# A hybrid attention block: first stacks and values loaded inside the projection, attention's results kept by token, the memory stage's first batch loaded inside attention

## What is computed

```python
qk = x @ w_attn.T + b_attn                      # x is the normalised input, v = x
q, k, v = (_heads(q), _heads(k), _heads(x))     # 16 heads of 8
scores = where(causal, einsum('bhqd,bhkd->bhqk', q, k) * scale, -inf)
y_ar = einsum('bhqk,bhkd->bhqd', softmax(scores), v)
e  = v[:, :, 1:, :] - y_ar[:, :, :-1, :]
qa = -leaky_relu(-q[:, :, 1:, :] * scale, 0.02)
ka = sigmoid(_heads(x[:, :-1] @ w_k2.T + b_k2) * scale * 0.02)
y_ma = einsum('bhqk,bhkd->bhqd', where(strictly_causal, qa @ ka.T, 0), e)
out = merge(y_ar) @ w_proj.T + merge(y_ma) @ w_proj.T + 2 * b_proj
```

## Time and profile before

| what | value |
|---|---|
| median of three runs | 1926.33 us |
| profiled execution | 1940.25 us, span 1938.2 us |
| TensorE busy | 1394.9 us (72%) |
| VectorE busy | 1283.7 us (66%) |
| GpSimd busy | 863.3 us (45%) |
| ScalarE busy | 833.6 us (43%) |
| mean granted TensorE clock | 0.829 of full speed |
| projection | 0 to 88.5 us |
| attention | 88.5 to 628.6 us |
| memory stage | 628.6 to 818.8 us |

### The profile page before, as it was taken

How to read it: one execution, slowest core, us unless ns; L and a number is a source line. 1 busy time by engine, 2 the same in 40 slices (tenths; PEclk the granted TensorE clock), 3 DMA queues, 4 the chain that set the end, 5 groups by cost and what they waited for, 6 DMA issues and landing times. The chain is left out here.

```text
span 1938.2 us, 29318 instructions
## 1 busy us (share of the span) xinstructions
PE 1394.9 (72%) x8975; PEld 721.5 (37%) x8976; DVE 1283.7 (66%) x2982; ACT 833.6 (43%) x1181; POOL 863.3 (45%) x761
## 2 busy tenths in 40 slices
PE   4459999999998488767598557586686545481992
PEld 1113333333332366644497222131131101351992
DVE  4567888888983144476233259999999998571333
ACT  3305666666666011122254267557466332120551
POOL 3401111121122333367366316876868665473662
PEclk9657999999999587878799778788797666796996
DMA  4721111111100765153232367785957763534335
GB/s 136 233 78 40 44 61 43 54 52 42 61 9 10 110 122 99 40 160 108 59 94 78 104 168 185 195 211 146 233 147 188 191 163 76 161 94 115 88 93 147
DMA packets 232076, 214.96 MB, mean 111 GB/s; under 512 B 66079, under 2 KB 201218, under 8 KB 229634
## 3 DMA queue, kind: packets, MB, share of 16 engines
q1 hardware_dynamic: 209934, 184.90, 37.6%
q0 software_dynamic: 9216, 19.02, 3.0%
q10 hardware_dynamic: 12800, 9.46, 1.6%
HBM read 149.46 MB, written 63.37 MB: 110 GB/s over the span
## 5 line engine op out<-in xcount | busy, mean ns | idle before, releaser
L772 ACT ACTIVATE attn_prob<-attn_ps_cols 128x1024 f32<-128x1024 f32 (+1 forms) x320 | 290.5, 940 | 231.1 <-PE attn_ps_cols L648 229.8
L2298 POOL TENSOR_TENSOR ssm_hc<-ssm_h,ssm_cb 128x1024 f32<-128x1024 f32 x128 | 301.4, 2356 | 169.8 <-DVE ssm_h L2281 122.3
L2281 DVE TENSOR_TENSOR_SCAN ssm_h<-ssm_decay,ssm_ps_u 128x1024 f32<-128x1024 f32 x128 | 292.6, 2286 | 17.2 <-DVE ssm_ps_u L2276 0.5
L798 POOL TENSOR_SCALAR_AFFINE_SELECT attn_prob<-attn_prob 128x512 f32<-128x512 f32 x128 | 81.2, 635 | 428.2 <-ACT attn_prob L772 428.2
L680 DVE CUSTOM_DVE_ANT_0 attn_ps_rows<-attn_ps_rows,const_mask_rows 128x384 f32<-128x384 f32 (+3 forms) x512 | 235.4, 521 | 42.6 <-PE attn_ps_rows L615 42.5
L615 PE MATMUL attn_ps_rows<-attn_ks,attn_qs 72*128 72x512 bf16 (+3 forms) x768 | 228.3, 351 | 42.3 <-DMA attn_qs<-parts_dram 29.1
L2232 PE MATMUL ssm_ps_u<-ssm_stack,ssm_spread 96*128 96x512 bf16 x256 | 100.3, 484 | 175.7 <-DVE ssm_h L2281 170.3
L2269 ACT ACTIVATE ssm_decay<-ssm_wide,ssm_aneg 128x1024 f32<-128x1024 f32 x128 | 146.0, 1146 | 179.0 <-DVE ssm_h L2281 120.6
L648 PE MATMUL attn_ps_cols<-attn_qs,attn_ks 75*128 75x512 bf16 (+3 forms) x768 | 194.4, 333 | 4.9 <-DMA attn_qs<-attn_nrows 4.1
L667 PE MATMUL attn_ps_o<-attn_prob,attn_vw 128*32 128x512 f32 (+3 forms) x1536 | 166.6, 506 | 0.3 <-POOL attn_prob L798 0.3
L685 DVE TENSOR_REDUCE attn_nm<-attn_ps_rows 128x1 f32<-128x512 f32 x256 | 157.7, 680 | 7.8 <-PE attn_ps_rows L615 7.8
(11 more groups left out here) (321 smaller groups left out, 2471.1 us busy)
## 6 DMA issues: line engine op xcount, KB each, us to landing
ssm_wide<-delta_dram SPq DMA_DIRECT2D x128, 512.0 KB, 6.4
attn_ks<-parts_dram SPq DMA_DIRECT2D x48, 192.0 KB
attn_qs<-parts_dram SPq DMA_DIRECT2D x48, 192.0 KB
parts_dram<-proj_parts SPq DMA_DIRECT2D x8, 768.0 KB, 3.8
ffn1e_x<-ex_dram SPq DMA_DIRECT2D x40, 130.0 KB, 2.3
ffn2e_x<-ex_dram SPq DMA_DIRECT2D x40, 130.0 KB, 2.2
split_dram<-ssm_parts SPq DMA_DIRECT2D x6, 768.0 KB, 4.4
ssm_stack<-split_dram SPq DMA_DIRECT2D x18, 256.0 KB, 4.3
```

What stands on the lines that cost most here:

```text
L772: nc.scalar.activation(prob[u % RING][:, heads[0]:heads[-1] + 1, 0:w], ps_cols[s % 2][:].rearrange("p b (x q) -> p (b x) q", x=len(heads) ...
L2281: nc.vector.tensor_tensor_scan(h[t % H_RING][:], decay[t % DECAY_RING][:], ps_u[t % 2][:], 0.0, ALU.mult, ALU.add).then_inc(scan_done, 1)
L2298: nc.gpsimd.tensor_tensor(hc[:, t % HC_RING, :], h[t % H_RING][:], cb[b % 2][:], ALU.mult).then_inc(hc_done, 1)
```

## The change

Three things are done. First, `qs`, `ks`, `vc` and their semaphores live in a holder `Lead` made before the projection. SP issues the stacks of groups 0 and 1 and the values of groups 0 and 1 between the last stores of the projection. Second, `yar` has the shape 4096 x 128, a row to a token: each `y` store writes 128-byte pieces 512 bytes apart, and `yt` is loaded by one DMA of 512-byte pieces. Third, a holder `Early` has the memory stage's weights and the buffers of its first batch. They are loaded by SP behind group 12 (weights, `kr`, `qr`) and group 13 (`kaT`, `yt`, `vs`, `qaT`, `x`). Besides, a stack is loaded one column step later (`cols_done` at `g * SPG + 1`).

```diff
+class Lead:
+    def __init__(self, nc, ctx):
+        self.m = m = Mem(nc, ctx, "lead")
+        self.qs = [m.sb(f"qs{k}", [SROWS, GH, T], BF16) for k in range(STACKS)]
+        self.ks = [m.sb(f"ks{k}", [SROWS, GH, T], BF16) for k in range(STACKS)]
+        self.vc = [m.sb(f"vc{k}", [P, BLK, GH * (HD + 1)]) for k in range(2)]
...
+    def load_stack(self, sp, dram, g, k):
...
+        for s in range(PARTS):
+            at = s * PARTS * HD
+            sp.dma_start(self.ks[k][at:at + PARTS * HD], split[1][g]).then_inc(self.k_loaded[k], 16)
+            sp.dma_start(self.qs[k][at:at + PARTS * HD],
+                         split[0][g, s].unsqueeze(0).broadcast_to([PARTS, HD, GH * T])).then_inc(self.q_loaded[k], 16)
...
                     store_parts(B - 2 + k // 2, k % 2)
+                    if k == 0:
+                        for half in range(2):
+                            sp.wait_ge(parts_stored[half], 16)
+                    if k < 2:
+                        lead.load_stack(sp, dram, k, k)
+                    if k == 2:
+                        for half in range(2):
+                            sp.wait_ge(vp_stored[half], 16)
+                            lead.load_values(sp, dram, half, half)
...
-        yar = dram["yar"].rearrange("g (c j p) n -> g c p j n", c=2, p=P)
+        yar = dram["yar"].rearrange("(b c j p) (g n) -> b g c p j n", b=B, c=2, p=P, g=GPB)
...
             if stack:
-                sp.wait_ge(cols_done, g * SPG)
+                sp.wait_ge(cols_done, g * SPG + 1)
...
-                load_stack(sp, 0, 0)
-                for k in range(2):
-                    sp.dma_start(vc[k][:], vp[0, k]).then_inc(v_loaded[k], 16)
-                load_stack(sp, 1, 1)
                 sp.wait_ge(ones_ready, 1)
...
+                    if g == GROUPS - 4:
+                        early.load_weights(sp, a)
+                        early.load_rows(sp, dram)
+                    if g == GROUPS - 3:
+                        for ch in range(2):
+                            sp.wait_ge(y_stored[ch], GPB * 16)
+                        early.load_tokens(sp, dram, a)
...
-            for g in range(GPB):
-                sp.dma_start(yt[k][:, :, g * GH * HD:(g + 1) * GH * HD], yar[i, g]).then_inc(y_loaded[k], 16)
+            sp.dma_start(yt[k][:], dram["yar"][i * T:(i + 1) * T, :].rearrange("(j p) d -> p j d", p=P)).then_inc(y_loaded[k], 16)
...
-                for i in range(B):
+                for i in range(1, B):
                     load_batch(sp, i)
```

More of the change, by code:

```diff
@@ L24 @@
 KROWS = COMBOS * HD
+SROWS = KROWS + PARTS
+STACKS = 4
 MROW = 96
@@ L549, in bank_free, with __init__, load_rows, load_weights @@
     return nth(g, same[-1] if same else -1)
-def attention(nc, dram, c):
+RTILES = 4
+class Early:
+    def __init__(self, nc, ctx):
+        self.m = m = Mem(nc, ctx, "early")
+        self.wrow, self.brow = m.sb("wrow", [P, P]), m.sb("brow", [P, P])
+        self.qr, self.kr = m.sb("qr", [P, GH, T]), m.sb("kr", [P, GH, T])
+        self.kaT, self.qaT = m.sb("kaT", [P, T]), m.sb("qaT", [P, T])
+        self.yt, self.vs, self.x = (m.sb(n, [P, BLK, D]) for n in ("yt", "vs", "x"))
+        self.w_loaded = m.sem("w_ld")
+        self.r_loaded, self.y_loaded, self.v_loaded, self.ka_loaded, self.qa_loaded, self.x_loaded = (
+            m.sem(n) for n in ("r_ld", "y_ld", "v_ld", "ka_ld", "qa_ld", "x_ld"))
+    def load_rows(self, sp, dram):
+        feature = [dram["fT"][q].rearrange("(g d r) (b t) -> b r d g t", g=GPB, d=HD, b=B) for q in range(2)]
+        for r in range(RTILES):
+            sp.dma_start(self.kr[32 * r:32 * r + HD], feature[1][0, r]).then_inc(self.r_loaded, 16)
+            sp.dma_start(self.qr[32 * r:32 * r + HD], feature[0][0, r]).then_inc(self.r_loaded, 16)
+    def load_weights(self, sp, a):
+        sp.dma_start(self.wrow[:], a["w_proj"]).then_inc(self.w_loaded, 16)
+        sp.dma_start(self.brow[:], a["b_proj"].rearrange("(o n) -> o n", o=1).broadcast_to([P, P])).then_inc(self.w_loaded, 16)
+    def load_tokens(self, sp, dram, a):
+        sp.dma_start(self.kaT[:], dram["fT"][1, :, 0:T]).then_inc(self.ka_loaded, 16)
+        sp.dma_start(self.yt[:], dram["yar"][0:T, :].rearrange("(j p) d -> p j d", p=P)).then_inc(self.y_loaded, 16)
+        sp.dma_start(self.vs[:], dram["xn"][1:T + 1, :].rearrange("(j p) d -> p j d", p=P)).then_inc(self.v_loaded, 16)
+        sp.dma_start(self.qaT[:], dram["fT"][0, :, 0:T]).then_inc(self.qa_loaded, 16)
+        sp.dma_start(self.x[:], a["x"][0:T, :].rearrange("(j p) d -> p j d", p=P)).then_inc(self.x_loaded, 16)
@@ L555, in attention @@
+def attention(nc, dram, c, lead, early, a):
     with ExitStack() as ctx:
         m = Mem(nc, ctx, "attn")
-        qs = [m.sb(f"qs{k}", [SROWS, GH, T], BF16) for k in range(STACKS)]
-        ks = [m.sb(f"ks{k}", [SROWS, GH, T], BF16) for k in range(STACKS)]
+        qs, ks, vc, q_loaded, k_loaded, v_loaded = lead.qs, lead.ks, lead.vc, lead.q_loaded, lead.k_loaded, lead.v_loaded
         ones = m.sb("ones", [PARTS, GH * T], BF16)
-        vc = [m.sb(f"vc{k}", [P, BLK, GH * (HD + 1)]) for k in range(2)]
@@ L574, in attention @@
         filled, passed, ones_ready, ones_stored = (m.sem(n) for n in ("filled", "passed", "ones_ready", "ones_st"))
-        q_loaded, k_loaded = ([m.sem(f"{n}{k}") for k in range(STACKS)] for n in ("q_ld", "k_ld"))
-        v_loaded, v_wide = m.pair("v_ld"), m.sem("v_wide")
+        v_wide = m.sem("v_wide")
         rows_done, rows_free = m.sem("rows_done"), m.sem("rows_free")
@@ L831, in _ @@
                     sp_group(sp, g, g % 4, g > 0, g + 1 < GROUPS, g + 3 < GROUPS,
[L832 removed]
+                             g + 2 < GROUPS)
+                    if g == GROUPS - 4:
[5 more added lines that the diff above has]
+                        early.load_tokens(sp, dram, a)
                 store_y(sp, GROUPS - 1, 1, nth(GROUPS - 1, RPP - 1) + 1)
@@ L879, in attention @@
         m.leave()
+        lead.m.leave()
 HALF = BLK // 2
-RTILES = 4
 AM_RING = 2
@@ L1182, in memory @@
         m.leave()
+        early.m.leave()
 EXPERTS, HIDDEN, TOP = 8, 256, 2
@@ L2627, in build @@
         routing_scratch(nc, m, dram, ("ffn1", "ffn2"))
-        project(nc, dram, c, {"x": rows, "w_attn": w_attn, "b_attn": b_attn, "w_k2": w_k2, "b_k2": b_k2})
-        attention(nc, dram, c)
-        memory(nc, dram, c, {"x": rows, "w_proj": w_proj, "b_proj": b_proj})
+        with ExitStack() as held:
+            early, rest = Early(nc, held), {"x": rows, "w_proj": w_proj, "b_proj": b_proj}
+            with ExitStack() as led:
+                lead = Lead(nc, led)
+                project(nc, dram, c, {"x": rows, "w_attn": w_attn, "b_attn": b_attn, "w_k2": w_k2, "b_k2": b_k2}, lead)
+                attention(nc, dram, c, lead, early, rest)
+            memory(nc, dram, c, early, rest)
         ffn(nc, dram, c, experts, "ffn1", dram["x1"], None)
```

61 lines of the change are left out of this document (28 added, 33 removed).

## The result

The kernel after the change takes 1912.14 us, the median of 8 runs (1905.66 to 1916.3). The kernel before, run beside it, takes 1933.43 us (8 runs, 1923.79 to 1941.78). The ratio is 0.9889 with a 95% interval of 0.9865 to 0.9913, that is 21 us less (17 to 26). The forecast was 36 us less and 1890 us; its range ended at 1912. Faster was right, the size was not. Of the gap of 22 us, 7 come from the kernel before, whose median of 8 lies above the median of three that the forecast stood on; the rest is the change itself.

What follows compares the result with a forecast made beforehand. Bound by DMA waits at both attention boundaries and in the memory stage; +8.4 - 21.0 - 8 - 9.2 - 6 = -35.8 us, taken from the median 1926.3, gives 1890 us, range 1863 to 1912.

Steps and rivals of the forecast that it cites:

- The first boundary: Projection to attention: early stacks hold up the last parts stores, attention starts at 116 instead of 88.5; net +8.4 us.
- the DMA share in the idle stretch: Sign before attention's start: compute engines idle with a DMA share near 0.19.
- The start of the memory stage: kr and qr are there, GpSimd is late next; first outputs 9.9 us after the start against 30.9: -21.0 us.
- The first batch: Memory stage, pace of the first batch: the low clock lasts some 15 us, the rest runs at full pace; -8 us taken.
- Batches 2 and 3: Memory stage: vs lands earlier, saving 4.6 us twice, -9.2, with 4 us of waiting left; clock another -6.
- its clock: Memory stage, batches 2 and 3: one of two low-clock spells goes as the idle gap before it halves; -6 us.
- the wait term: Memory stage, batches 2 and 3: VectorE's waits for vs in make_e shrink by 4.6 us each, -9.2 us.
- its forecast of 146: Sign: the memory stage lasts about 146 us instead of 190; wrong if longer than 165.
- inside attention: Later stacks, early loads of the memory stage and y stores cost nothing: 0 taken, early loads up to +4 us.
- the first rival: First boundary: stores pass the stacks, the projection ends at 88.5 as now; -63.3 us, 1863; chance 0.13.
- the third: First boundary: the stacks' 8 KB pieces slow down beside the projection's stores; net +38 us, 1964; chance 0.04.
- The second rival: Memory stage: the clock stays low, so only waits go; -22.6 us, 1904; chance 0.20.

Runs made afterwards that it cites:

- e1: The changed kernel with its loads of stacks 0 and 1 and the values put back to attention's start; ratio to the kernel before 0.9825.
- e4: The changed kernel without kr and qr loads for batches 2 and 3, whose products use batches 0 and 1; ratio to before 0.9785, memory stage 134.8 us.
- e6: The changed kernel with each kr and qr pair of batches 2 and 3 issued only when the pair before has landed; ratio to before 0.9937.
- e13: The changed kernel with kr and qr loads of partitions 64-71 and 96-103, batches 1 to 3, issued by ScalarE's queue; ratio to before 0.9843, stage 136.6 us.
- e14: As e13, but ScalarE issues partitions 32-39 and 96-103, SP 0-7 and 64-71; ratio to before 0.992, memory stage 165.1 us.
- e8: e9 with kr and qr of batches 2 and 3 issued pair by pair as in e6; ratio to before 0.9841, memory stage 166.4 us.
- e9: e7 with stack 0 issued in the projection behind the last parts store; ratio to the kernel before 0.9805, memory stage 154.7 us.
- e11: e9 with yt and vs of a batch issued ahead of kr and qr; ratio to the kernel before 0.9862, memory stage 165.0 us.
- e12: e11 with kr and qr issued pair by pair in batches 1, 2 and 3; ratio to the kernel before 0.9832, memory stage 155.4 us.
- e15: e7 with the two-queue kr and qr loads of e13; ratio to the kernel before 0.9769, memory stage 145.0 us.
- e7: e1 with stack 2 issued behind the store of group 0's maxima, not ahead of it; ratio to the kernel before 0.9801.
- e10: The changed kernel with kr and qr of batches 2 and 3 issued in two steps of four DMAs; ratio to the kernel before 0.9888.

## Why the prediction was wrong in size

**The first boundary was right, step by step.** The loads hold up the stores behind them for as long as they take. Attention's first instruction was put at 116 and came at 115.12; the first maximum at 120.4 and came at 121.99 (VectorE was ready near 119.5 and waited 2.48 us for TensorE's first rows); the columns net +8.4 and came +9.4, with no wait for `nrows`. The `parts` wait of the last unit was 10.61 us (over 10 was expected). e1 shows the cost by itself. One sign was missed: the DMA share in the idle stretch was put near 0.19, and only parts of the stretch show that. Which of the 16 engines carry the stacks no run shows; 0.19 shows how many.

**The start of the memory stage was nearly right.** First outputs came 11.2 us behind the start (9.9 expected): -19.6 instead of -21.0. GpSimd was the one waited for, as said; but it waited 1.25 us for `make_e` itself, since TensorE's first products stand 4.3 us behind the stage's start (637.41) and not 2.5.

**The first batch** took 683.93 - 644.35 = 39.6 us for eight tiles, -5.5 instead of -8. The low clock lasted until 668.2, 23.8 us from the first outputs and not the 15 us assumed, and a hole with the releaser issue of 2.54 us came at 657.53.

**The step that failed is "Batches 2 and 3" with its clock.** It was put at -9.2 and -6, and said "4 us of waiting stay". From the outputs of tile 8 to those of tile 31 the stretch went from 107.7 to 99.6 us, -8.1 instead of -15.2. The waits for `vs` went altogether, further than forecast, but TensorE did not get the gain. Its two long idle stretches were 8.84 and 6.01 us before (behind `make_e`) and are 3.90 and 7.36 us now (releaser issue): -3.6 us where -9.2 stood. The other -4.5 is what the clock gave, where -6 stood: one spell was to go, and instead both stayed, shorter (12.5 and 7.1 us instead of 14.1 each). So the larger miss is the wait term, not the clock. The step took the whole gain of VectorE's waits for TensorE's and did not ask what else shares the engines with `kr` and `qr`; it had no term for TensorE's own instructions, which come over them too. The 7.1 us between -15.2 and -8.1 are the largest part of the 10.9 us by which the stage missed its forecast of 146. e4 shows that the holes hang on these loads, e6 that they go when the pieces are not queued, e13 against e14 that the loads are slow for the partitions they go to.

**What else the profile shows.** The -4.9 us inside attention is not the change's. It all lies in group 0, where the granted clock rises from 1.2 to 2.4 GHz earlier or later: after, near 166 us, 13 us behind the first columns; before, near 170, 27 us behind them, though TensorE is busy without a break from 148 to 172. The two windows, after and before:

```profile
163.00:169.00 6.00, 6.00 (x35) 1.95 (x35) 4.38 (x8) 1.85 (x3) 1.68 (x3) 0.72 0.19 81
```

```profile
166.00:172.00 6.00, 6.00 (x28) 1.96 (x30) 3.42 (x12) 2.54 (x3) 0.00 (x0) 0.66 0.01 3
```

From the first columns to the memory stage it takes 480 us in after, e8, e9, e11, e12, e14 and e15, and 485 to 487 in before, e1 to e7, e10 and e13. e6, e10, e13 and e14 have the first boundary of the kernel after, and e15 that of e7, so the same boundary gives either time and this is a matter of the execution. Without it and the 3.8 us of the stages behind, the profiles give +9.4 - 33.3 = -23.9 us, which fits the medians' -21. The forecast of -35.8 came close to the profiled -32.6 only by that luck.

**The rivals.** The stores did not pass the stacks: the first rival is out. The stacks did not slow down: the third is out. The second rival, a clock that stays low, gave -22.6 us, close to the measured -21. That it fits is in part luck: later tiles kept low spells, but shorter ones and behind holes of another kind, and the waits that it took as gone came back as these.

## What to carry to other kernels

When a wait for a load goes, look at which other transfers use the same engines, TensorE's own instructions among them: they show as idle time with the releaser "issue" in the middle of a run of like instructions, with a packet of the instruction queue just before its end. Loads put ahead of stores on the same few engines can delay the end of the stage by nearly their full length: two stacks of 1.2 MB on three engines, 29 us by their rate, moved it from 88.5 to 115.1 us here. Where a load goes to few partitions, count the bytes against the time: if it is far below the other loads with the DMA engines full, changing the order may only move the wait, as it did here, and it is worth trying to load two groups of partitions 64 apart side by side, from two queues.

## What was not expected of the hardware

- 8 partitions at a time (and the 8 that lie 32 further) take some 52 GB/s with eight engines on them: 1.05 MB of `kr` and `qr` in 20 us, pieces of 4 KB in about 620 ns (median) where those of `kaT` take 159.
- A packet of 16 KB of the instruction queue started 16.15 us after the one before (713.88, 730.03) while such pieces were queued, and TensorE was idle for 7.36 us; in e11 such holes reached 10.90.
- Memory stages of kernels that differ only at the first boundary vary (156.9, 157.9, 153.3, 151.2 us), and so do their holes in batches 1 to 3 (3.90 and 7.36 us; 3.36 and 5.15; 3.31 and 7.67; 3.36, 1.60 and 1.75). A single profile is not enough to size such a term.
